# The last three steps of a gated delta scan as a program of their own

## What is computed

```python
def step(St, inp):                       # one token; St is 128x128 for each image
    qt, kt, vt, at, bt = inp
    Sk = einsum('bij,bj->bi', St, kt)
    Sn = a * (St - b * Sk[:, :, None] * kt[:, None, :]) + b * vt[:, :, None] * kt[:, None, :]
    ot = einsum('bij,bj->bi', Sn, qt)
...
h = h + linear(rmsnorm(scan) * silu(gate))          # attention with its residual
x = layernorm(h)
gh = relu(x @ gfc1_w.T + gfc1_b)
g = (gh @ gfc2_w.T + gfc2_b).mean(axis=1)           # the mean over all tokens of an image
W1m = W1 + einsum('be,efd->bfd', g, tv_W1)          # W2m, b1m and b2m likewise
out = relu(x @ W1m.T + b1m) @ W2m.T + b2m
h = h + layernorm(x + out) * lng + lnb
```

## Time and profile before

| | us |
|---|---|
| median of 3 runs | 867.81 (864.57 to 872.59) |
| the profiled execution | 872.72 |
| its span, first to last instruction | 870.8 |
| body of j = 24 begins on TensorE | 621.9 |
| g is there, the first weight sum starts | 676.9 |
| the first hidden product starts | 687.05 |
| the first unit's products end | 694.32 |

### The profile page before, as it was taken

The page is one execution under the profiler, slowest core; times in us unless marked ns, Lnnn a source line. Parts: engine busy times, 40 slices in busy tenths (PEclk is TensorE's granted clock), DMA queues, the critical chain, the costliest instruction groups (busy, mean ns, idle before and its releaser), DMA issues. The chain is left out here.

```text
span 870.8 us, 31506 instructions
## 1 busy us (share of the span) xinstructions
PE 822.8 (94%) x11990; PEld 646.3 (74%) x11990; DVE 647.0 (74%) x2316; ACT 500.5 (57%) x1775; POOL 364.1 (42%) x530
## 2 busy tenths in 40 slices
PE   7689999999999999999999999999886999999996
PEld 5467777877787877787778787778664777777775
DVE  4357888888888888888888888888743876767444
ACT  1435566566666656666666665666533366666554
POOL 3122333233333233323333323333211288888875
PEclk9989999999999999999999999999976799999999
DMA  2000222222212011111111111110102133333331
GB/s 58 16 12 13 49 56 61 49 61 62 59 38 56 27 35 33 36 25 37 37 37 34 36 27 34 33 31 21 27 26 60 61 97 110 119 117 123 115 109 43
DMA packets 78660, 45.35 MB, mean 52 GB/s; under 512 B 20357, under 2 KB 69803, under 8 KB 78511
## 3 DMA queue, kind: packets, MB, share of 16 engines
q1 hardware_dynamic: 77663, 42.80, 17.7%
q10 hardware_dynamic: 848, 0.54, 0.2%
HBM read 23.69 MB, written 19.63 MB: 50 GB/s over the span
## 5 line engine op out<-in xcount | busy, mean ns | idle before, releaser
L1589 ACT ACTIVATE work<-bank,b1mix 128x512 f32<-128x512 f32 x96 | 66.0, 687 | 58.3 <-PE bank L1681 58.2
L1707 PEld LDWEIGHTS bank<-work 128*128 128x128 f32 x768 | 89.5, 192 | 11.5 <-issue 11.5
L1707 PE MATMUL bank<-work 128*128 128x128 f32 x768 | 89.6, 275 | 0.0
L1681 PE MATMUL bank<-work 128*128 128x512 f32 x192 | 86.5, 593 | 0.0
L473 ACT ACTIVATE work<-bank 128x512 f32<-128x512 f32 x50 | 29.9, 597 | 98.4 <-PE bank L1103 98.4
L656 POOL TENSOR_SCALAR var2e<-mv 128x4 f32<-128x4 f32 x25 | 5.7, 229 | 192.1 <-DVE mv L832 192.1
L1102 PE MATMUL bank<-SA,work 128*128 128x256 f32 x200 | 69.5, 430 | 0.0
L1103 PE MATMUL bank<-SB,work 128*128 128x256 f32 x200 | 61.2, 388 | 0.0
L1054 PEld LDWEIGHTS bank<-work 32*32 32x32 f32 x3200 | 35.4, 107 | 34.0 <-issue 28.5
L1681 PEld LDWEIGHTS bank<-work 128*128 128x128 f32 x192 | 34.6, 190 | 34.6 <-issue 34.2
L1506 DVE TENSOR_TENSOR work<-bank,work 128x512 f32<-128x512 f32 x24 | 16.6, 692 | 56.2 <-PE bank L1707 56.1
(11 more groups left out here) (238 smaller groups left out, 2376.2 us busy)
## 6 DMA issues: line engine op xcount, KB each, us to landing
hn_kept<-work SPq DMA_DIRECT2D x25, 256.0 KB, 2.3
hnT_kept<-work SPq DMA_DIRECT2D x25, 256.0 KB, 2.3
work<-hnT_kept SPq DMA_DIRECT2D x25, 256.0 KB, 2.9
work<-hn_kept SPq DMA_DIRECT2D x25, 256.0 KB, 3.1
out_dram<-work SPq DMA_DIRECT2D x24, 256.0 KB, 2.5
tv<-in_L_ffn_tv_W_dram SPq DMA_DIRECT2D x16, 256.0 KB
work<-r_kept SPq DMA_DIRECT2D x25, 98.0 KB
work<-in_x_dram SPq DMA_DIRECT2D x23, 102.0 KB
```

The lines of the kernel that those rows point to most:

```text
L1589: ins = nc.scalar.activation(hid[f][:, :], ps[:, :], ACT.Relu, bias=b1mix[:, of[0], f:f + 1])
L1681: ins = mm(ps[:, :], w1T[of[0]][:, f, :], ghT[par][:, :, :].rearrange("p t c -> p (t c)"), start=True, stop=True)
L1707: ins = mm(by4(bank[2 + par])[:, t, :], hid[f][:, t * C:(t + 1) * C], w2T[of[t]][:, f, :], start=(f == 0 and t == 0), stop=(f == FB - 1), ...
```

## The change

The loop ends with j = 23, and each engine gets a `drain()` with its own order for the rest. Level functions take the step as an argument; they are otherwise as before (on TensorE a no-op fewer at level 5, and the waits of levels 5 and 6 in another order). In the drain:

- the keys and queries of step 24 are multiplied by the state as soon as step 23's state is there, between levels 4 and 5, and the state update of step 23 moves up between levels 3 and 4. Queries by state go to bank 3, no longer to bank 6;
- step 24's own state update, which nobody reads, is left out;
- the norm and gate stages of steps 22 and 23 stand after the solve of step 24, among the waits of its output;
- `keep_busy(n)` issues n products of the identity by itself into bank 2, which nobody reads: 39 of them ahead of g, 2 behind;
- the last gate product takes 65 columns of each image, not 128;
- the sums over the first 24 steps are reduced ahead of the last relu; one product of the weight mixing (L1653) and the four of the merged norm weights (L1446, L1447) are issued earlier;
- SP fetches the tiles of the first two feed-forward units in the drain.

```diff
-        first, last = -2, STEPS + 1
+        first, last = -2, STEPS - 2
+        END = STEPS - 1
```

VectorE's list of the drain:

```diff
+            def drain():
+                c, s = END - 1, END
...
+                new_blocks(1, s)
+                keys_corrected(c)
...
+                grow(1, s)
+                residual(END - 2, 6)
+                new_blocks(2, s)
...
+                grow(2, s)
+                norm2_statistics(END - 2)
+                new_blocks(3, s)
+                grow(3, s)
+                dve.wait_ge(dm_ps, c + 1)
+                for b in range(NB):
+                    ins = nc.vector.scalar_tensor_tensor(state[:, b, :], state[:, b, :], g_raw[c % 2][:, NB + b:NB + b + 1], by4(bank[5])[:, b, :],
+                                                         ALU.mult, ALU.add)
+                ins.then_inc(state_ready, 1)
+                new_blocks(4, s)
...
+                grow(4, s)
+                output(c)
+                new_blocks(5, s)
+                keys_corrected(s)
+                output_variance(c)
+                new_blocks(6, s)
+                output_gated(c)
+                norm2(END - 2)
+                output(s)
+                residual(END - 1, 3)
+                output_variance(s)
+                norm2_statistics(END - 1)
+                output_gated(s)
+                norm2(END - 1)
+                residual(END, 6)
+                norm2_statistics(END)
+                norm2(END)
```

TensorE's list:

```diff
+            def drain():
+                c, s = END - 1, END
+                def keep_busy(n):
+                    for _ in range(n):
+                        mm(bank[2][:, 0:D], ident[:, :], ident[:, :], start=True, stop=True)
...
+                pe.wait_ge(state_ready, c)
+                by_state(kT, 5, c, km_ps)
+                level_blocks(1, s)
...
+                output_rows(END - 2, 6)
+                level_update(1, s)
...
+                keep_busy(3)
+                level_blocks(2, s)
+                solve(c)
+                level_update(2, s)
...
+                by_state(qT, 3, c, qm_ps)
+                level_blocks(3, s)
...
+                    ins = mm(by4(bank[5])[:, b, :], kd[c % 2][:, b, :], Zn[:, b, :], start=True, stop=True)
+                ins.then_inc(dm_ps, 1)
+                level_update(3, s)
...
+                inside(c)
+                level_blocks(4, s)
+                keep_busy(3)
+                level_update(4, s)
+                pe.wait_ge(state_ready, s)
+                by_state(kT, 5, s, km_ps)
+                level_blocks(5, s)
...
+                by_state(qT, 3, s, qm_ps)
...
+                level_update(5, s)
+                keep_busy(4)
...
+                level_blocks(6, s)
+                keep_busy(3)
+                level_update(6, s)
+                keep_busy(2)
+                solve(s)
+                output_tokens(c)
+                keep_busy(1)
...
+                inside(s)
...
+                output_rows(c, 3)
+                gate_tokens(END - 2)
+                keep_busy(3)
+                gate_hidden(END - 2)
+                keep_busy(4)
+                output_tokens(s)
+                keep_busy(1)
...
+                output_rows(s, 6)
+                gate_tokens(END - 1)
+                keep_busy(2)
+                gate_hidden(END - 1)
+                pe.wait_ge(Zn_ready, STEPS)
+                ffn["tensor_early"](pe)
+                keep_busy(5)
+                gate_tokens(END)
+                keep_busy(2)
+                gate_hidden(END)
+                pe.wait_ge(h1_ready, END)
+                ffn["tensor_start"](pe)
+                keep_busy(6)
```

VectorE's reduction ahead of g:

```diff
+        dve.wait_ge(A["relu_ready"], STEPS - 1)
+        nc.vector.tensor_reduce(gh_kept[:, :], A["gate_sums"][:, 0:STEPS - 1, :].rearrange("p s b -> p b s"), AX.X, ALU.add).then_inc(gh_part, 1)
...
-        nc.vector.tensor_reduce(gh[:, :], A["gate_sums"][:, :, :].rearrange("p s b -> p b s"), AX.X, ALU.add).then_inc(gh_ready, 1)
+        nc.vector.tensor_tensor(gh[:, :], gh_kept[:, :], A["gate_sums"][:, STEPS - 1, :], ALU.add).then_inc(gh_ready, 1)
```

More of the change, by code:

```diff
@@ L586, in _ @@
             iterations(body)
+            drain()
             ffn["scalar"](act)
@@ L764, in body, with grow @@
+            def grow(k, s):
+                dve.wait_ge(Xps_done, 6 * s + k)
+                nc.vector.tensor_tensor(Xd[s % 2], by32(X_ps), Xd[s % 2], ALU.add).then_inc(X_ready, 1)
+                dve.wait_ge(X_ready, 5 * s + k + 1)
+                nc.vector.transpose(Yd[s % 2].rearrange("p b c -> p (b c)"), Xd[s % 2].rearrange("p b c -> p (b c)")).then_inc(Y_ready, 1)
             def body(j, par):
                 p = 1 - par
[L767 to L792, removed]
                 if on(j, LH):
@@ L1027, in fold_weights, with level_blocks @@
                 ins.then_inc(gate_ps, 1)
+            def level_blocks(k, s0):
+                par = s0 % 2
+                if k <= 5:
+                    pe.wait_ge(Y_ready, 5 * s0 + k)
+                else:
+                    pe.wait_ge(Yd_kept, s0 + 1)
+                    pe.wait_ge(Y5_ready, s0 + 1)
+                need(pe, blk_ready, 6 * s0 + k - 1)
+                if k == 1:
+                    need(pe, X6_ready, s0)
+                apart(pe)
+                for b in range(NB):
+                    if k < 5:
+                        for r in range(SUBS):
+                            ins = mm(by32(blk_ps)[sub(r), b], Bm[par][sub(r), b, sub(r)], Yd[par][sub(r), b, :], start=True, stop=True)
+                    elif k == 5:
+                        for r in (0, 64):
+                            ins = mm(by32(blk_ps)[r + 32:r + 64, b], Bm[par][r:r + 32, b, r + 32:r + 64],
+                                     Yd[par][r:r + 32, b, :], start=True, stop=True)
+                    else:
+                        ins = mm(by64(bank[7])[64:128, b], Bm[par][0:64, b, 64:128], Y[0:64, b, :], start=True, stop=True)
+                ins.then_inc(blk_ps_done, 1)
@@ new lines, in level_update @@
+            def level_update(k, s0):
+                par = s0 % 2
+                pe.wait_ge(blk_ready, 6 * s0 + k)
+                if k == 6:
+                    pe.wait_ge(X5_ready, s0 + 1)
+                    pe.wait_ge(Xd_kept, s0 + 1)
+                apart(pe)
+                if k == 5:
+                    for b in range(NB):
+                        ins = mm(by32(bank[1])[32:64, b], Xd[par][32:64, b, :], N5[32:64, b, :], start=True, stop=True)
+                    ins.then_inc(Y5ps_done, 1)
+                for b in range(NB):
+                    if k < 5:
+                        for r in range(SUBS):
+                            ins = mm(by32(X_ps)[sub(r), b], newblk[k][sub(r), b, :], Xd[par][sub(r), b, :], start=True, stop=True)
+                    elif k == 5:
+                        for r in (0, 64):
+                            ins = mm(by32(X_ps)[r:r + 32, b], N5[r + 32:r + 64, b, :],
+                                     Xd[par][r + 32:r + 64, b, :], start=True, stop=True)
+                    else:
+                        ins = mm(by64(X_ps)[0:64, b], N6[64:128, b, :], X[par][64:128, b, 64:128], start=True, stop=True)
+                ins.then_inc(Xps_done, 1)
@@ L1032, in body @@
                 s1, s0, c, h, e = j + LF, j + LI, j + LC, j + LH, j + LE
[L1034 to L1089, removed]
@@ L1315, in make_ffn @@
     ln_ready = sem("ln_ready")
+    gh_part = sem("gh_part")
     gh_ready = sem("gh_ready")
@@ L1643, in tensor, with keep_busy @@
         mm = nc.tensor.matmul
-        tensor_early(pe)
+        def keep_busy(n):
+            for _ in range(n):
+                mm(bank[2][:, 0:D], ident[:, :], ident[:, :], start=True, stop=True)
         pe.wait_ge(gh_ready, 1)
```

339 lines of the change are left out of this document (299 added, 40 removed).

## The result

The changed kernel takes **856.19 us** in the median (852.93 to 859.03, 7 runs) and the kernel before, beside it, 864.57 (860.60 to 872.59, 7 runs): a ratio of **0.9891 [0.9862, 0.9921]**. Timed a second time, beside later experiments: 855.68 against 865.15, 0.9879 [0.9845, 0.9914]. The forecast was 857.0 and 10.8 us less than before; the medians differ by 8.4 and 9.5.

A forecast was written before the change was run, and what follows sets the result against it. No engine bounds the drain; a chain of single steps does, lengthened by TensorE's order and clock. With g 12.5 us earlier, 0.4 gained and 2.1 lost, 10.8 us off the 867.81 median gave 857.0, range 853 to 861.

The forecast's parts named there:

- The levels: Step 24's levels in the drain: 3.2 us shorter, from a full clock and a gate product moved out.
- Copy to output product: Drain, from the last copy to step 24's output: 8.0 us shorter.
- the solve's place: Behind the last copy: work ahead of step 24's solve done earlier or moved behind it, 5.0 us gained.
- From there to g: Drain, from step 24's output to g: 2.3 us shorter.
- The reserve of 1.0 for hand-overs: Drain: some forty new hand-overs between engines, put at 1.0 us against the gain.
- The first unit: Weight mixing and first feed-forward unit: 0.4 us gained, 2.1 lost to a clock fall, 1.7 given back.
- The line that this unit would stay at about 17 us: Sign of being right: first weight sum to the first unit's end still about 17 us.
- the clock did not fall in the drain: Rival that the clock falls in the drain too: 5.3 us of gain remain, 862.5 us; chance 0.22.
- It did not hold in the first unit: Rival that the clock holds in the first unit as well: 2.1 us more gain, 854.9 us; chance 0.17.
- TensorE as the bound, slower: Rival: the 39 constant products ahead of g make TensorE the drain's bound, 20 us slower, 888; chance 0.06.
- The change does what it says: Opposing rival: levels run no faster and waits behind keep the rest, 2 us of gain remain, 866; chance 0.05.
- the row: Weight mixing, earlier trace: a VectorE sum under a GpSimd add took 1.383 instead of 0.485, 0.9 us more.

The follow-up runs named there:

- e1: The changed kernel without its 41 constant products, new order kept: 855.23 us, ratio 0.9872 to the kernel before.
- e8: The changed kernel with GpSimd's first three adds behind VectorE's 24 weight sums and without any constant product: 854.07 us, ratio 0.9856.
- e5: The changed kernel with keys and queries of step 24 by state put behind the levels again: 857.88 us, ratio 0.9886.
- e9: The same edit of the changed kernel as e5, timed again: 861.00 us beside 855.68 for the changed kernel, ratio 0.9935.
- e3: The changed kernel with GpSimd's first three adds held until VectorE's 24 weight sums are done: 851.56 us, ratio 0.9824.
- e7: The changed kernel with GpSimd's first three adds behind VectorE's 24 weight sums and without the four constant products ahead of level 6: 851.14 us, ratio 0.9822.

## Why the prediction was right

Each step of the sum was seen in the traces, and the time came within 0.8 us of the median. The gain came less close: 10.8 forecast, 8.4 and 9.5 measured. Point by point:

- **The levels**: forecast 3.2 us shorter, 23.32 - 19.14 = 4.2 against the profile that it was worked out from, 2.6 against the second. The constant products among them were put at 0.6; with all of them out the levels are 0.86 shorter (e1, e8).
- **Copy to output product**: forecast 8.0, measured 18.43 - 10.09 = 8.3. Its pieces too: the solve comes 5.1 nearer to the copy (5.0), the product inside 2.5 nearer to the solve (2.2 and a quarter), and the way from there to the output product 0.7 shorter (0.9 less 0.3). What the forecast couldn't know: 3.4 of these 8.3 are a fall of the clock that the second profile of before doesn't have (15.04 there). Against that profile, at the full clock on both sides, the three pieces are 3.7, 1.5 and -0.2: 5.0 is what the order itself is worth here, and the 5.0 that the sum put down to the solve's place held 1.4 of clock.
- **From there to g**: forecast 2.3, measured 2.9 against either profile. Its terms were not tested one by one. In e1, without constant products, this stretch takes 11.93 us (646.50 to 658.43), so 1.3 of the 2.9 come without them and 1.6 with them.
- **The reserve of 1.0 for hand-overs** was not needed.
- **The first unit**: forecast 0.4 gained and 2.1 lost to the clock; measured 0.7 longer than before in two profiles and 2.2 in the third (1.0 and 2.5 against the second profile of before). The adds cost 2.8 (forecast 2.7), the wait was 3.2 (3.6), the clock 0.9 to 2.4 (2.1). The line that this unit would stay at about 17 us didn't fit the forecast's own sum, which makes it 17.4 + 1.7 = 19.1 to this unit's own end; 18.0 to 19.4 came (to the second unit's start, some 0.2 earlier).

Against its own profile the sum was 4 us short (10.8, measured 14.7), against the second over by 1.4 (9.4). It met the medians because that profile was of a long execution and the sum kept its distance of 4.9 to the median, while the fall of the clock that made it long went away with the change. And it started from the median of three runs, 867.81; seven runs gave 864.57, so a start 3.2 too high met a gain 2.4 too large. That the time came within 0.8 us is luck of size, not of mechanism: a drain whose clock falls at changing places should have been read in more than one profile.

Of the rivals, the clock did not fall in the drain in any of three profiles of the changed kernel, but only just: move the two state products behind the levels (e5, e9) or take out the constant products (e1, e8) and it falls. It did not hold in the first unit in any of the three. TensorE as the bound, slower: it is busy 18.13 of 19.14 us among the levels, and the cost is the 0.86 above. The change does what it says. One reading of the prediction was loose: what the prediction gives as TensorE's work before the fall, 2.48 of 5 us, straddles it; in the part ahead, 625.00 to 627.30, it is 0.77 of 2.30 us.

On the exclusive lock of the shared port pair (the Trainium skill, page SBUF — State Buffer, section "SBUF: two separate sides"): the three adds of 1.26, 1.45 and 1.44 us lengthened VectorE's sums by 6.39 - 3.61 = 2.78 in all, 0.93 each, as the earlier trace rows had it. The sum was right to go by the row. But the row doesn't speak against an exclusive use, as the prediction took it to. Here are the three long sums of the changed kernel, one by one:

```profile
667.86 1.50 DVE L1827 SCALAR_TENSOR_TENSOR work<-tv,g_all,work 128x256 f32<-128x256 f32 x1
669.39 1.37 DVE L1827 SCALAR_TENSOR_TENSOR work<-tv,g_all,work 128x256 f32<-128x256 f32 x1
670.80 1.37 DVE L1827 SCALAR_TENSOR_TENSOR work<-tv,g_all,work 128x256 f32<-128x256 f32 x1
```

The adds end at 669.08, 670.48 and 671.88, the sums at 669.36, 670.76 and 672.16: each 0.28 us behind an add. The next add has begun on record by then (669.03, 670.44) and takes 1.45 and 1.44 us, not 1.26. It looks as if sums and adds take turns, as that rule of the Trainium skill would have it; what fails is the step from that rule to a loss of 1.27 us for each sum. Part of a sum's own 0.485 us may pass while it waits for the add; that is an inference from these ends, and no run here tests it.

## What to carry to other kernels

Filler work that holds TensorE's clock is worth only what the next wait leaves of it: here it brought g forward by 2.0 us and lost 0.8 of that in two profiles and all of it in a third at a wait for another engine, until the adds that lengthened this wait were moved (one wait on GpSimd, in e3 and e7; e7 is 4.5 us below the changed kernel). At the tail of a pipeline look first for steps that need only old state and take them off the chain behind the last dependence; they fill the pauses ahead of it as well. Where the clock falls at changing places, profile the kernel twice before pricing a stretch.

## What the runs showed of the hardware that was not expected

- The same wait of TensorE can bring its clock down or not: 3.20 us ahead of the third hidden product, the clock fell in three profiles of the changed kernel and in e9, and held in e5 with a wait of 3.19.
- An add on GpSimd grows beside VectorE too, when a sum is under way: of three adds among the 128x256 sums the first took 1.26 us, as one alone, the others 1.45 and 1.44; beside two 128x512 sums in e3, which took 3.32 us instead of 1.54, adds took 1.56 and 1.71. There it cost nothing, since nobody waited for that pair.
